# A fused AdaLN attention and FP4 feed-forward block: quantizer slots from a table, an identity product issued earlier, and steps in a new order

## The chip, the cores and the metric

The kernel runs on one core of one Trainium2 chip. The metric is the device time of one execution in microseconds (us), median of the runs shown. The core's engines are TensorE (PE in the rows; its weight loads PEld), VectorE (DVE), ScalarE (ACT), GpSimd (POOL) and SyncE (SP). Each engine works through its own instruction stream in order, and they meet through semaphores.

## The reference, cut to what matters

The input x is 4 batches of 1024 tokens of 128 features in float32. `c` gives six modulation vectors per batch.

```
h = layernorm(x) * (1 + ca) + sa
q, k = l2norm(heads(h Wq)), l2norm(heads(h Wk));  v = heads(h Wv)      # 16 heads of 8
beta, fast, slow = sigmoid(h Wb), sigmoid(h Wfd + bfd), sigmoid(h Wsd + bsd)
flux = clip(sigmoid(silu(k beta Wtf1 + btf1) Wtf2 + btf2), .01, .99)
M_fast, M_slow = sums over all tokens of (k beta weight)^T (v beta), weight = exp(suffix sum of log decay)
x = x + ga * ((alpha q M_fast + (1 - alpha) q M_slow) Wo),  alpha = 0.5 + 0.3 flux
h = layernorm(x) * (1 + cb) + sb
f = silu(q4(h) q4(w_gate)^T) * (q4(h) q4(w_up)^T)                      # 352 wide
x = x + gb * (q4(f) q4(w_down)^T)
```

`q4` quantizes to FP4 and back: in blocks of 16 values, scale = max|.|/6, the quotient rounded to the grid 0, .5, 1, 1.5, 2, 3, 4, 6, times the scale.

## The kernel before, in words

The 4096 tokens are worked on as 16 pairs (of 2 times 128 tokens), four pairs to a batch. A table, `ORDER`, gives for each of four engines a written list of steps such as `F1:12` (step F1, pair 12); the engine's program is that list and nothing reorders it. A step's name stands on each engine that takes part in it.

- First part, all pairs: `XN` normalizes, `PX` transposes, `PP` is the product with all attention weights (496 columns) and its copies out by ScalarE, and per batch the gates: `GA` (ScalarE, functions exp and ln), `GD`, `GS`, `GE` (silu and tanh), `V0` to `V3` (the state), `GG`. `MB` makes the modulation vectors, `W1`, `W2`, `W3` quantize and transpose the feed-forward weights.
- Second part, per pair i: `O1`, `O2`, `O3` (attention output, added to x), `L1` (second layer norm; its result goes to `q_x` columns 704 to 959), quantize, `N4` (transpose), `F1` (gate and up products, silu, the product of both into `q_x` columns 0 to 703), quantize, `F3` (transposes), `F4` (down product plus x, copy out, store).
- The quantizer works by slots. Slot s takes the columns that it has in one go: `Q` (VectorE: block maximum, scale, reciprocal), `QR` (GpSimd: times reciprocal), `QA` (ScalarE: absolute value into the one PSUM tile `q_A`), `QT` (VectorE: two instructions that round), `QO` (GpSimd: times scale). `q_x`, `q_r`, `q_o` have two buffers, taken by s mod 2. The norm of pair i is in slot i+4 and its feed-forward vector in slot i+6, so a slot has norm i with vector i-2. Of the 18 slots (4 to 21) the first two hold a norm alone (256 columns), the last two a vector alone (704 columns), 14 hold both (960 columns).

PSUM: three banks `pa` for results that ScalarE copies out, taken in turn in the order of TensorE's list, two banks `pv` for those that VectorE reads, one `pg` for the gates. A product waits until the bank three places earlier in that list is free. ScalarE's function tables hold either the exp/ln set or the silu/tanh set; where the list needs the other set, line 526 loads it.

Of the kernel before, what the change touches and what calls it, by code (L numbers as in the profile page):

```python
# [11 lines left out]
P = 128  # L12
# [66 lines left out]
        P0:0 XN:0 MV:0 XN:1 XN:2 XN:3 SB:0 P0:1 P0:2 PP:0 PP:1 PP:2 GA:0 P0:3 PP:3 W0:0 GB:0 PP:4 W1:0 PP:5 GK:0
        PP:6 W2:0 GE:0 PP:7 GF:0 PP:8 GA:1 GB:1 GY:0 PP:9 GG:0 GK:1 GA:2 PP:10 PP:11 O1:0 O1:1 GE:1 O1:2 GF:1  # L80
        O3:0 GB:2 O3:1 GY:1 L1:0 PP:12 O1:3 GK:2 GG:1 L1:1 Q:4 O3:2 QT:4 O3:3 Q:5 L1:2 GF:2 O1:4 PP:13 L1:3 GE:2
        PP:14 O1:5 PP:15 QT:5 F1:0 GA:3 Q:6 GB:3 O3:4 O1:6 GK:3 GG:2 QT:6 L1:4 O3:5 F1:1 GY:2 Q:7 L1:5 F1:2 Q:8
        QT:7 O1:7 O3:6 GE:3 QT:8 O1:8 L1:6 F1:3 GF:3 O1:9 Q:9 F1:4 Q:10 QT:9 O3:7 O3:8 L1:7 QT:10 F1:5 Q:11 GG:3
# [1140 lines left out]
```

## Time and profile before

| | us |
|---|---|
| median of 3 runs (lowest, highest) | 214.57 (213.33, 214.69) |
| the profiled execution's own time | 214.73 |
| its span in the trace | 213.0 |
| busy in the span: PE, DVE, ACT, POOL | 185.1, 174.6, 144.6, 152.9 |

The rows below are of that one execution. A row of a timeline gives start, duration, engine, line, operation, output and input, how many instructions it merges, and in brackets the idle time before it with the instruction that ended it. The steps of the list can be told by their lines: 952 to 960 are `Q`, 475 is `QR`, 691 `QA`, 968 and 971 `QT`, 487 `QO`, 982 the VectorE half of `F1`, 1177 and 714 are `F3`, 1187 and 1189 `F4`.

### The profile page before, as it was taken

What the parts mean: (1) busy time and instruction counts of PE and PEld (TensorE: products, weight loads), DVE (VectorE), ACT (ScalarE), POOL (GpSimd) and SP (SyncE); (2) the same over time, 40 slices, a digit from 0 to 9 for tenths busy, and PEclk for the clock granted to TensorE, in tenths of its full rate; (3) what the DMA queues carried; (4) which work ended last, traced back from release to release, by engine and by line L of the source; (5) the groups of instructions that cost most, each with busy time, mean ns of one, the idle gap of its engine ahead of it and who ended that gap; (6) DMA issues with size and microseconds to landing.
All of it is one profiled execution on the core that took longest, in us unless ns stands there. A gap on an engine that the chain in (4) does not pass through costs nothing.

```text
span 213.0 us, 3498 instructions
## 1 busy us (share of the span) xinstructions
PE 185.1 (87%) x948; PEld 134.6 (63%) x948; DVE 174.6 (82%) x436; ACT 144.6 (68%) x326; POOL 152.9 (72%) x187
## 2 busy tenths in 40 slices
PE   2699959699999999879669999989999996989973
PEld 1544426366787748539538777868786683875863
DVE  3795998956898999999999999899998896876730
ACT  2369898998998999969753637655726456653741
POOL 6367353797688878979997975977867967666530
PEclk9999987999999999999999999999999999999999
DMA  6980000000000000000000100010001000010011
GB/s 166 247 211 5 0 2 0 5 0 0 0 5 0 0 0 2 0 0 5 25 0 0 29 0 25 2 29 0 25 11 42 0 25 25 3 51 26 3 49 49
DMA packets 11499, 5.66 MB, mean 27 GB/s; under 512 B 1684, under 2 KB 11352, under 8 KB 11480
## 3 DMA queue, kind: packets, MB, share of 16 engines
q1 hardware_dynamic: 11168, 5.31, 9.1%
q8 instruction: 8, 0.13, 0.3%
q10 hardware_dynamic: 312, 0.13, 0.2%
q14 instruction: 11, 0.09, 0.1%
HBM read 3.34 MB, written 2.10 MB: 26 GB/s over the span
## 4 chain that ended last, share of the span: by engine, by line
PE 49%; ACT 18%; issue 13%; POOL 9%; DVE 6%; DMA 2%; SPq 0%; POOLq 0%; DVEq 0%; ACTq 0%
PE pa L1089 10%; PE pa L1166 6%; PE pv L1168 5%; PE pa L1189 4%; PE pv L1130 4%; POOL q_o L487 3%; PE pg L1113 3%; POOL q_r L475 3%; PE pa L1177 3%; PE pa L1139 3%; DMA wmod_sb<-in_L_wmod_dram 2%; ACT L526 2%; PE pv L1149 2%; ACT xn L680 2%; PE pa L1187 2%
## 5 line engine op out<-in xcount | busy, mean ns | idle before, releaser
L475 POOL TENSOR_TENSOR q_r<-q_x,q_rs 128x960 f32<-128x960 f32 (+2 forms) x18 | 29.6, 1644 | 14.4 <-DVE q_rs L960 14.3
L1089 PE MATMUL pa<-wcat,hT 128*128 128x496 f32 x64 | 32.2, 631 | 5.4 <-ACT sq L606 3.6
L487 POOL TENSOR_TENSOR q_o<-q_r,q_sp 128x960 f32<-128x960 f32 (+2 forms) x18 | 29.5, 1642 | 7.3 <-DVE q_r L971 6.4
L1166 PE MATMUL pa<-guT,hqT 128*128 128x352 f32 x64 | 25.3, 477 | 4.8 <-ACT hqT L697 4.7
L1189 PE MATMUL pa<-wdg,fqT 128*128 128x128 f32 x192 | 26.7, 275 | 0.0
L706 ACT ACTIVATE sgl<-pa 128x352 f32<-128x352 f32 x32 | 14.5, 461 | 15.1 <-PE pa L1166 12.9
L1168 PE MATMUL pv<-guT,hqT 128*128 128x352 f32 x64 | 24.3, 462 | 0.3 <-DVE oc L913 0.3
L438 POOL TENSOR_TENSOR vs<-kvg,cw 128x256 f32<-128x256 f32 x32 | 20.0, 651 | 5.8 <-DVE cw L864 5.8
L1189 PEld LDWEIGHTS pa<-wdg,fqT 128*128 128x128 f32 x192 | 24.0, 192 | 0.0
L1089 PEld LDWEIGHTS pa<-wcat,hT 128*128 128x128 f32 x64 | 12.0, 205 | 16.8 <-ACT sq L606 7.1
L691 ACT ACTIVATE q_A<-q_r 128x960 f32<-128x960 bf16 (+2 forms) x18 | 16.0, 888 | 8.3 <-POOL q_r L475 5.3
L982 DVE TENSOR_TENSOR q_x<-sgl,pv 128x352 f32<-128x352 f32 x32 | 15.7, 511 | 5.9 <-PE pv L1168 5.0
L968 DVE SCALAR_TENSOR_TENSOR q_x<-q_A,q_r 128x960 f32<-128x960 f32 (+2 forms) x18 | 18.5, 1026 | 2.5 <-ACT q_A L691 2.4
L952 DVE TENSOR_REDUCE q_am<-q_x 128x60 f32<-128x960 f32 (+2 forms) x18 | 18.7, 1039 | 1.0 <-POOL q_x L466 0.6
L971 DVE SCALAR_TENSOR_TENSOR q_r<-q_A,q_x 128x960 f32<-128x960 f32 (+2 forms) x18 | 18.8, 1046 | 0.6
L1166 PEld LDWEIGHTS pa<-guT,hqT 128*128 128x128 f32 x64 | 11.0, 189 | 11.3 <-ACT hqT L697 7.4
L1130 PE MATMUL pv<-wm,hT 128*128 128x256 f32 x64 | 16.5, 385 | 1.9 <-DVE q_x L982 1.7
L714 ACT ACTIVATE fqT<-pa 128x384 f32<-128x384 f32 x32 | 13.9, 486 | 6.1 <-PE pa L1177 6.1
L603 ACT ACTIVATE kvg<-pa 128x368 f32<-128x368 f32 x32 | 15.2, 475 | 3.8 <-PE pa L1089 3.1
L1168 PEld LDWEIGHTS pv<-guT,hqT 128*128 128x128 f32 x64 | 12.0, 190 | 7.6 <-DVE oc L913 1.2
L680 ACT ACTIVATE xn<-x_all,nmrb,rstdb 128x128 f32<-128x128 f32 x32 | 13.9, 485 | 3.2 <-DVE nmrb L941 3.0
L462 POOL TENSOR_TENSOR q_x<-xn,mb 128x256 f32<-128x256 f32 x16 | 11.8, 739 | 5.5 <-issue 5.1
(149 smaller groups left out, 447.5 us busy)
## 6 DMA issues: line engine op xcount, KB each, us to landing
out_dram<-x_all SPq DMA_DIRECT2D x16, 128.0 KB, 1.8
x_all<-in_L_attn_x_dram SPq DMA_DIRECT2D x3, 512.0 KB, 5.6
x_all<-in_L_attn_x_dram SPq DMA_DIRECT2D x2, 256.0 KB, 3.1
wmod_sb<-in_L_wmod_dram SPq DMA_DIRECT2D x1, 256.0 KB, 5.7
wraw<-in_L_ffn_w_down_dram SPq DMA_DIRECT2D x1, 176.0 KB, 4.5
wmod_sb<-in_L_wmod_dram SPq DMA_DIRECT2D x1, 128.0 KB, 5.2
wraw<-in_L_ffn_w_gate_dram SPq DMA_DIRECT2D x1, 128.0 KB, 3.2
wraw<-in_L_ffn_w_up_dram SPq DMA_DIRECT2D x1, 128.0 KB, 2.9
```

The source lines that it names most:

```text
L438: g.tensor_tensor(vs[:, t].rearrange("p a (h d) -> p a h d", d=DK), vt.unsqueeze(1).to_broadcast([P, 2, H, DK]), cw[:, t].unsqueeze(3).to_ ...
L475: g.tensor_tensor(blocks(q_r[:, s % 2, c]), blocks(q_x[:, s % 2, c]), spread(q_rs[:, s % 2, n]), ALU.mult)\
L487: g.tensor_tensor(blocks(q_o[:, s % 2, c]), blocks(q_r[:, s % 2, c]), spread(q_sp[:, s % 2, n]), ALU.mult)\
L680: a.activation(xn2[:, i % 2, k, :], x_all[:, b, 2 * j + k, :], ACT.Identity, scale=rstdb[:, i % 2, k:k + 1], bias=nmrb[:, i % 2, k:k + 1]) ...
L952: v.tensor_reduce(q_am[:, r, n], blocks(q_x[:, r, c]), axis=AX.X, op=ALU.max, apply_absolute_value=True)\
L968: v.scalar_tensor_tensor(q_x[:, r, c], q_A[:, c], MAGIC_FLOOR, q_r[:, r, c], ALU.max, ALU.add)\
L971: v.scalar_tensor_tensor(q_r[:, r, c], q_A[:, c], MAGIC_FLOOR, q_x[:, r, c], ALU.max, ALU.subtract, reverse1=True).then_inc(S["q_q"], 1)
L1089: te.matmul(bank_a(("PP%d" % k, i))[:, 0:NCAT], hT[:, b, 2 * j + k, :], wcat[:, :], start=True, stop=True).then_inc(S["a_full"], 1)
L1130: last = te.matmul(t[:, k * 2 * D:(k + 1) * 2 * D], hT[:, b, 2 * j + k, :], wm[:, b % 2, :], start=True, stop=True)
L1166: te.matmul(bank_a(("G%d" % k, i))[:, 0:I], lhs, guT[:, 0, :], start=True, stop=True)\
L1168: te.matmul(bank_v(("U%d" % k, i))[:, 0:I], lhs, guT[:, 1, :], start=True, stop=True)\
L1189: last = te.matmul(t[:, k * D:(k + 1) * D], fqT[:, (2 * i + k) % 4, ch * P:(ch + 1) * P], wdg[:, b % 2, ch, :], start=False, stop=(ch == 2))
```

## The change: what it does, and the diff

1. The slots come from a table, `SLOTS`. Norms 0 and 1 are alone in slots 0 and 1, slots 2 to 13 hold norm i with vector i-2 as before, norms 14 and 15 now stand alone in slots 14 and 15, and vectors 12 to 15 alone in slots 16 to 19. There are 20 slots: four of 256 columns, twelve of 960, four of 704. `before(s, part)` finds the slot that last used the same buffer for that part.
2. In `F4` TensorE's identity product of the first half (it adds x) no longer waits for ScalarE's copies of `F3`; the first half then waits for copy FT0 and the second for FT1. Before, all waited for FT1.
3. All four lists of `ORDER` are new. Of the table one line for one engine stands here.

```
-        P0:0 P0:1 KC:0 XN:4 XN:5 XN:6 P0:2 XN:7 P0:3 GO:0 XN:8 XN:9 GC:0 XN:10 GB:0 V0:0 GO:1 XN:11 V1:0 V2:0
+        KC:0 P0:0 P0:1 XN:4 XN:5 XN:6 P0:2 XN:7 GC:0 XN:8 XN:9 GO:0 GB:0 XN:10 XN:11 V0:0 V1:0 V2:0 V3:0 GF:0
...
-Q_NORM, Q_FFN = 4, 6
...
+        SLOTS = [(i, i - 2 if i >= 2 else None) for i in range(14)] + [(14, None), (15, None)] + [(None, i) for i in range(12, 16)]
+        norm_slot = {n: s for s, (n, _) in enumerate(SLOTS) if n is not None}
+        ffn_slot = {f: s for s, (_, f) in enumerate(SLOTS) if f is not None}
+
         def quant_span(s):
-            lo = 0 if s - Q_FFN >= 0 else QF0
-            return slice(lo, QCOLS if s - Q_NORM < PAIRS else QF0), slice(...)
+            n, f = SLOTS[s]
+            lo, hi = 0 if f is not None else QF0, QCOLS if n is not None else QF0
+            return slice(lo, hi), slice(lo // BLOCK, hi // BLOCK)
+
+        def before(s, part):
+            return max((p for p in range(s) if p % 2 == s % 2 and SLOTS[p][part] is not None), default=None)
...
             def QO(s):
-                if 0 <= s - 2 - Q_NORM < PAIRS:
-                    pool.wait_ge(S["a_full"], slot_a[("HQT", s - 2 - Q_NORM)] + 1)
-                if s - 2 - Q_FFN >= 0:
-                    pool.wait_ge(S["a_full"], slot_a[("FT1", s - 2 - Q_FFN)] + 1)
+                for part, bank in ((0, "HQT"), (1, "FT1")):
+                    p = before(s, part)
+                    if SLOTS[s][part] is not None and p is not None:
+                        pool.wait_ge(S["a_full"], slot_a[(bank, SLOTS[p][part])] + 1)
...
             def F4(i):
                 v_done(("Y", i))
-                a_done(("FT1", i))
-                pe.wait_ge(S["wdg"], b + 1)
                 for k in range(2):
                     te.matmul(t[:, k * D:(k + 1) * D], ident[:, :], x_all[:, b, 2 * j + k, :], start=True, stop=False)
+                    a_done(("FT%d" % k, i))
+                    if k == 0:
+                        pe.wait_ge(S["wdg"], b + 1)
                     for ch in range(3):
```

How the lists move the work is shown at three places. First, ScalarE at the first gate step of batch 0, between the copies of `PP:3` and of the pairs after it, before:

```order
L606 ACTIVATE sq<-pa 128x256
L590 ACTIVATE hT<-pa,colmod 128x256
L555 ACTIVATE mb<-pa 128x512 x4
L590 ACTIVATE hT<-pa,colmod 128x256
L603 ACTIVATE kvg<-pa 128x368
```

and with the change:

```order
L611 ACTIVATE sq<-pa 128x256
L531 ACT_TABLE_LOAD
L620 ACTIVATE eg<-zb 128x384
L623 ACTIVATE rn<-ss 128x256
L625 ACTIVATE rn<-rn,ln 128x256
L629 ACTIVATE lg<-eg 128x384
L631 ACTIVATE lg<-lg 128x384
L635 ACTIVATE lf<-lg,tiny 128x256
L560 ACTIVATE mb<-pa 128x512 x4
L595 ACTIVATE hT<-pa,colmod 128x256
```

The table load and the six activations of `GA:0` now stand ahead of the four copies of `MB:0`; before they came behind these, the `hT` copies of `PX:6` and `PX:7`, `PP:4` and `WQ:0`.

Second, VectorE's last steps, from the vector product of pair 12 on, before:

```order
L982 TENSOR_TENSOR q_x<-sgl,pv 128x352 x2
L952 TENSOR_REDUCE q_am<-q_x 128x60
L957 TENSOR_SCALAR q_sp<-q_am 128x60
L960 RECIPROCAL q_rs<-q_sp 128x60
L982 TENSOR_TENSOR q_x<-sgl,pv 128x352 x2
L952 TENSOR_REDUCE q_am<-q_x 128x60
```

and with the change:

```order
L961 RECIPROCAL q_rs<-q_sp 128x16
L981 TENSOR_TENSOR q_x<-sgl,pv 128x352 x2
L967 SCALAR_TENSOR_TENSOR q_x<-q_A,q_r 128x256
L970 SCALAR_TENSOR_TENSOR q_r<-q_A,q_x 128x256
L953 TENSOR_REDUCE q_am<-q_x 128x16
L958 TENSOR_SCALAR q_sp<-q_am 128x16
L961 RECIPROCAL q_rs<-q_sp 128x16
L953 TENSOR_REDUCE q_am<-q_x 128x44
L958 TENSOR_SCALAR q_sp<-q_am 128x44
L961 RECIPROCAL q_rs<-q_sp 128x44
L967 SCALAR_TENSOR_TENSOR q_x<-q_A,q_r 128x256
L970 SCALAR_TENSOR_TENSOR q_r<-q_A,q_x 128x256
```

The norms of pairs 14 and 15 are small slots of their own (16 blocks) beside vector 12's slot (44 blocks), where two slots of 60 blocks stood.

Third, TensorE's last step, `F4:15`, with the semaphores that its instructions wait for, before:

```order
L1187 MATMUL pa<-x_all,ident 128x128 [waits s_a_free,s_wdg,s_v_free]
L1189 MATMUL pa<-wdg,fqT 128x128 x3
L1187 MATMUL pa<-x_all,ident 128x128
L1189 MATMUL pa<-wdg,fqT 128x128 x3
L130 UNCONDITIONAL_BRANCH
```

and with the change:

```order
L1184 MATMUL pa<-x_all,ident 128x128 [waits s_v_free,s_a_free]
L1189 MATMUL pa<-wdg,fqT 128x128 [waits s_wdg,s_a_free]
L1189 MATMUL pa<-wdg,fqT 128x128 x2
L1184 MATMUL pa<-x_all,ident 128x128
L1189 MATMUL pa<-wdg,fqT 128x128 [waits s_a_free]
L1189 MATMUL pa<-wdg,fqT 128x128 x2
L130 UNCONDITIONAL_BRANCH
```

The wait for the copies (s_a_free of FT0 and FT1) has moved from the identity product to the three products behind it.

## Rows read from the trace of the kernel before

**Rows 1.** The page's first part: busy us of each engine, share, instructions.

```profile
PE 185.1 (87%) x948; PEld 134.6 (63%) x948; DVE 174.6 (82%) x436; ACT 144.6 (68%) x326; POOL 152.9 (72%) x187
```

**Rows 2.** Windows of 20 us: length, busy of each engine (instructions), granted clock, DMA.

```profile
20.00:40.00 20.00, 15.07 (x45) 7.89 (x45) 18.46 (x45) 18.15 (x40) 8.86 (x15) 0.91 0.00 0
40.00:60.00 20.00, 19.78 (x88) 13.50 (x87) 14.53 (x32) 18.71 (x47) 16.66 (x27) 1.00 0.01 1
60.00:80.00 20.00, 19.77 (x92) 14.27 (x91) 18.00 (x61) 18.46 (x49) 16.30 (x26) 1.00 0.00 1
80.00:100.00 20.00, 17.64 (x92) 13.40 (x91) 19.45 (x45) 16.87 (x34) 17.56 (x20) 1.00 0.00 1
...
180.00:200.00 20.00, 18.39 (x111) 13.96 (x110) 14.89 (x24) 11.50 (x26) 12.49 (x11) 1.00 0.08 21
```

**Rows 3.** Timeline of TensorE, 20 to 42 us: MB:0 and two waits.

```profile
19.32 3.67 PE L1061 MATMUL pa<-wmod_sb,scB 128*128 128x512 f32 x8
...
31.19 2.02 PE L1089 MATMUL pa<-wcat,hT 128*128 128x496 f32 x2 [2.65 <-ACT sq L606]
...
39.51 1.90 PE L1089 MATMUL pa<-wcat,hT 128*128 128x496 f32 x4 [1.74 <-ACT hT L590]
```

**Rows 4.** Windows of TensorE around the first of these waits: busy, granted clock, DMA.

```profile
29.00:31.00 2.00, 0.00 (x0) 0.94 0.00 0
31.00:32.00 1.00, 0.81 (x1) 0.50 0.00 0
...
34.00:35.00 1.00, 1.00 (x8) 0.91 0.00 0
```

**Rows 5.** Timeline of ScalarE: step GA:0 with its table load.

```profile
26.00 0.29 ACT L546 ACTIVATE wqT<-pa 128x128 f32<-128x128 f32 x1
26.30 1.28 ACT L526 ACT_TABLE_LOAD   x1
27.60 0.52 ACT L615 ACTIVATE eg<-zb 128x384 f32<-128x384 f32 x1
...
29.99 0.51 ACT L630 ACTIVATE lf<-lg,tiny 128x256 f32<-128x256 f32 x1
```

**Rows 6.** Timeline of VectorE in the tail: products of F1, slots 20 and 21.

```profile
179.34 0.52 DVE L982 TENSOR_TENSOR q_x<-sgl,pv 128x352 f32<-128x352 f32 x1 [1.22 <-PE pv L1168]
...
194.33 0.52 DVE L982 TENSOR_TENSOR q_x<-sgl,pv 128x352 f32<-128x352 f32 x1 [0.61 <-PE pv L1168]
194.88 0.89 DVE L952 TENSOR_REDUCE q_am<-q_x 128x44 f32<-128x704 f32 x1
...
196.02 0.43 DVE L960 RECIPROCAL q_rs<-q_sp 128x44 f32<-128x44 f32 x1
...
199.82 0.83 DVE L968 SCALAR_TENSOR_TENSOR q_x<-q_A,q_r 128x704 f32<-128x704 f32 x1
...
202.46 0.89 DVE L968 SCALAR_TENSOR_TENSOR q_x<-q_A,q_r 128x704 f32<-128x704 f32 x1 [0.89 <-ACT q_A L691]
...
203.39 0.89 DVE L971 SCALAR_TENSOR_TENSOR q_r<-q_A,q_x 128x704 f32<-128x704 f32 x1
```

**Rows 7.** Timeline of VectorE in slot 4, a norm alone.

```profile
67.30 0.42 DVE L952 TENSOR_REDUCE q_am<-q_x 128x16 f32<-128x256 f32 x1
...
67.97 0.25 DVE L960 RECIPROCAL q_rs<-q_sp 128x16 f32<-128x16 f32 x1
...
69.37 0.42 DVE L968 SCALAR_TENSOR_TENSOR q_x<-q_A,q_r 128x256 f32<-128x256 f32 x1
69.83 0.42 DVE L971 SCALAR_TENSOR_TENSOR q_r<-q_A,q_x 128x256 f32<-128x256 f32 x1
```

**Rows 8.** Timeline of the last steps: F4:14, F3:15, F4:15 and the copy out.

```profile
204.81 0.46 PE L1187 MATMUL pa<-x_all,ident 128*128 128x128 f32 x2 [0.84 <-ACT fqT L714]
...
206.67 0.82 PE L1177 MATMUL pa<-ident,q_o 128*128 128x128 f32 x6
...
207.20 0.87 ACT L714 ACTIVATE fqT<-pa 128x384 f32<-128x384 f32 x2
...
208.32 0.46 PE L1187 MATMUL pa<-x_all,ident 128*128 128x128 f32 x2 [0.84 <-ACT fqT L714]
...
210.38 0.38 ACT L720 ACTIVATE x_all<-pa 128x256 f32<-128x256 f32 x1 [2.31 <-PE pa L1189]
```

More of the change, by code:

```diff
@@ L77 @@
         F3:15 F4:15""",
     "vector": """
[L79 to L83, printed above, removed]
@@ L459, in L1 @@
                 pool.wait_ge(S["xn2"], 2 * i + 2)
-                if i >= 2:
-                    pool.wait_ge(S["q_q"], nth(i + Q_NORM - 2))
-                g.tensor_tensor(q_x[:, (i + Q_NORM) % 2, QF0:QCOLS].rearrange("p (t d) -> p t d", t=2), xn2[:, i % 2], mb[:, b, 2, :].unsqueeze(1).to_broadcast([P, 2, D]),
+                if before(norm_slot[i], 0) is not None:
+                    pool.wait_ge(S["q_q"], nth(before(norm_slot[i], 0)))
+                g.tensor_tensor(q_x[:, norm_slot[i] % 2, QF0:QCOLS].rearrange("p (t d) -> p t d", t=2), xn2[:, i % 2], mb[:, b, 2, :].unsqueeze(1).to_broadcast([P, 2, D]),
                                 ALU.mult).then_inc(S["u"], 1)
                 pool.wait_ge(S["u"], i + 1)
-                h2 = q_x[:, (i + Q_NORM) % 2, QF0:QCOLS].rearrange("p (t d) -> p t d", t=2)
+                h2 = q_x[:, norm_slot[i] % 2, QF0:QCOLS].rearrange("p (t d) -> p t d", t=2)
                 g.tensor_tensor(h2, h2, mb[:, b, 1, :].unsqueeze(1).to_broadcast([P, 2, D]), ALU.add).then_inc(S["h2"], 1)
             def QR(s):
-                if nth(s) < 1:
-                    return
                 c, n = quant_span(s)
@@ L944, in Q @@
             def Q(s):
-                if nth(s) < 1:
-                    return
                 r, (c, n) = s % 2, quant_span(s)
-                if s - Q_FFN >= 0:
-                    dve.wait_ge(S["v_free"], slot_v[("U1", s - Q_FFN)] + 1)
-                if s - Q_NORM < PAIRS:
-                    dve.wait_ge(S["h2"], s - Q_NORM + 1)
+                if SLOTS[s][1] is not None:
+                    dve.wait_ge(S["v_free"], slot_v[("U1", SLOTS[s][1])] + 1)
+                if SLOTS[s][0] is not None:
+                    dve.wait_ge(S["h2"], SLOTS[s][0] + 1)
                 v.tensor_reduce(q_am[:, r, n], blocks(q_x[:, r, c]), axis=AX.X, op=ALU.max, apply_absolute_value=True)\
@@ L974, in F1 @@
             def F1(i):
-                r = (i + Q_FFN) % 2
-                if i + Q_FFN - 2 >= Q_NORM:
-                    dve.wait_ge(S["q_q"], nth(i + Q_FFN - 2))
+                r = ffn_slot[i] % 2
+                if before(ffn_slot[i], 1) is not None:
+                    dve.wait_ge(S["q_q"], nth(before(ffn_slot[i], 1)))
                 for k in range(2):
@@ L1153, in N4 @@
             def N4(i):
-                pe.wait_ge(S["q_o"], nth(i + Q_NORM))
+                pe.wait_ge(S["q_o"], nth(norm_slot[i]))
                 t = bank_a(("HQT", i))
                 for k in range(2):
-                    last = te.transpose(t[:, k * D:(k + 1) * D], q_o[:, (i + Q_NORM) % 2, QF0 + k * D:QF0 + (k + 1) * D], ident[:, :])
+                    last = te.transpose(t[:, k * D:(k + 1) * D], q_o[:, norm_slot[i] % 2, QF0 + k * D:QF0 + (k + 1) * D], ident[:, :])
                 last.then_inc(S["a_full"], 1)
@@ L1171, in F3 @@
             def F3(i):
-                pe.wait_ge(S["q_o"], nth(i + Q_FFN))
+                pe.wait_ge(S["q_o"], nth(ffn_slot[i]))
                 for k in range(2):
@@ L1176, in F3 @@
                         o = k * I + CH[ch]
-                        last = te.transpose(t[:, ch * P:(ch + 1) * P], q_o[:, (i + Q_FFN) % 2, o:o + P], ident[:, :])
+                        last = te.transpose(t[:, ch * P:(ch + 1) * P], q_o[:, ffn_slot[i] % 2, o:o + P], ident[:, :])
                     last.then_inc(S["a_full"], 1)
```

69 lines of the change are left out of this document (34 added, 35 removed).

## The prediction, made before the changed kernel ran

> **What bounds the kernel now.** I read the page's busy totals first, then windows of 20 us, then each engine's timeline where the windows show a gap. By the totals [rows 1] TensorE has the most work, 185.1 of 213.0 us, and VectorE 174.6, too close to name one bound for all. The windows [rows 2] tell the stages apart. From 40 to 80 us TensorE is busy 39.55 of 40 us and ScalarE 37.17: nothing that isn't taken off TensorE helps there, and ScalarE has 2.83 us to spare. From 80 us on VectorE is nearest to full (19.45 of 20), TensorE waits 2.36 us in 20. From 180 us on neither is full (VectorE 14.89 of 20): what limits there is the way round, from one quantizer slot through `N4`, `F1` and the next-but-one slot. The page's chain of waits hops between all four engines there, which says the same.
>
> In the start stretch, 20 to 40 us, TensorE is idle 4.93 us [rows 2], most of it in two waits: 2.65 us while ScalarE runs the gate step `GA:0`, and 1.74 us behind `GS:0` [rows 3]. After the first the granted clock is 0.50 until about 34 us [rows 4]: the 1.2 GHz level instead of 2.4, after two microseconds with no product at all. Some 3 us of products at half speed lost about 1.5 us.
>
> **The change, term by term.** All sums start from the profiled execution: span 213.0, own time 214.73, which is 0.16 above the median of 214.57.
>
> *The slots of the tail.* Before, norms 14 and 15 wait to be quantized with vectors 12 and 13, so `F1:14` can't begin before vector 12 exists, though it doesn't need it. With the change they go alone. I count VectorE's new list from its first product of `F1:12`, which starts at 179.34 [rows 6], since all ahead of it is the same in kind. Prices: `F1`, two products paced by TensorE 0.52 + 0.61 + 0.52 = 1.65, or 1.09 where TensorE is ahead (both 0.52 and a start gap, an estimate from the same row); `Q` of a vector alone 194.88 to 196.45, 1.57; its `QT` 0.83 and 0.89 back to back, 199.82 to 201.57, 1.75 [rows 6]; `Q` of a norm alone 67.30 to 68.22, 0.92, and its `QT`, 69.37 to 70.25, 0.88 [rows 7]. The list reads F1:12, QT:14, Q:15, Q:16, QT:15, which is 1.65 + 0.88 + 0.92 + 1.57 + 0.88 = 5.90; then three times F1, Q, QT, which is 3 x (1.09 + 1.57 + 1.75) = 13.23; then the wait for `QA` (there is one `q_A`) 0.89 and the last `QT` 1.82 (202.46 to 204.28) [rows 6]. Together 21.84: the last `QT` ends at 201.18 instead of 204.28, **3.1 us earlier**. `Q:14` adds 0.92 ahead of `F1:12`, in the 1.22 us that VectorE idles there; if that cover is gone (GpSimd late with norm 14's `L1`), it costs up to 0.92. This sum has VectorE never waiting otherwise. TensorE is not full there either, beside VectorE's 4.41 us per vector (`F1`, `F3`, `F4` and `N4`, of which `F4` takes 1.78 by the next term), and GpSimd's `QR` and `QO` of a vector are about as long as `Q` and `QT` together less the reduction; each hop between them can still show. Bounds: 0 (all of it returned as waits, since VectorE gets more slots to do, each with its own fixed part: 0.92 + 0.88 for 256 columns against 1.57 + 1.75 for 704) and 4.0. I take 3.1 here and keep 1.0 off as a margin below.
>
> *The identity product.* In `F4:15` the first product starts at 208.32, 0.25 us after the second copy ended at 207.20 + 0.87 = 208.07; the eight products issue in 1.78 us (F4:14 starts at 204.78 by its weight load, F3:15 follows at 206.56 in the same way; the rows of the products are 204.81 and 206.67) [rows 8], 0.22 each. The first copy ends about 0.43 before the second. Now the first half goes at 207.64 + 0.25 = 207.89 without its identity product, ends at 208.56, the second identity product at 208.78, the last three at 209.45 instead of 210.07: **0.6 us** for `F4:15`, and **0.6** more for `F4:14`, because `F3:15` stood behind it on TensorE: its input came from the `QT` that ended at 204.28 plus `QO` and was there by 205.8, yet it began at 206.67 [rows 6, 8]. For the 14 pairs before, the product is work that fills an idle moment where there is one and costs nothing where there isn't. Bounds 0.6 and 1.3; I take 1.2.
>
> *The order at the start.* `WK:0` moves behind `CM:0`: one small copy and transpose in front of the first `PX`, at most 0.3 us. `GA:0` moves in front of the copies of `MB:0`. By its rows it holds ScalarE from 26.30 to 30.50, 4.2 us [rows 5]. `MB:0` has four products in 3.67 us [rows 3], and three banks: TensorE can run three, some 2.7 us, and then waits for a copy that stands behind `GA:0`. The wait is then some 3 us in place of 2.65. At the old place of `GA:0` no wait remains, so the net is 0 to +0.6, and I take +0.3. At `GS:0`, `WQ:0` and the copies of `PP:7` now stand ahead of it, so TensorE has `GE:0` and `PP:8` to do while ScalarE is away: of the 1.74 us wait [rows 3] about half should go, -0.9 (bounds 0 and -1.7).
>
> *Two more table loads.* The new ScalarE list changes the function set 12 times, the old one 10. A load is 1.28 us [rows 5]: 2.57 us more on ScalarE before 80 us, where it has 2.83 us to spare and TensorE none [rows 2]. `W3:0` (nine copies) leaves that stretch for the one behind `N4:0`, which makes room. Hidden fully 0, not at all +2.6; I take half, +1.3. The rows show the load beginning as the copy before it ends (26.29) and the exp 0.02 us behind it [rows 5].
> The Trainium skill, "ScalarE: Activation LUTs", section "What ACT_TABLE_LOAD costs", gives a switch as a load of 1283 ns plus a drain of about 1380 ns, 2.66 us in all. By it the two loads would be 5.3 us and this term up to 2.7 us larger; the trace agrees on the load and shows no drain here.
>
> *The rest of the order.* The middle, 80 to 180 us, is rearranged by a few places everywhere. VectorE is nearly full there and its work is unchanged, so I give it 0, with bounds of -2 and +2 (half of what TensorE idles in the window from 80, on either side, twice over).
>
> Sum: -3.1 + 1.0 (hops) - 1.2 + 0.3 + 0.3 - 0.9 + 1.3 = -2.3. The terms that I halved (table loads, `GS:0`) lean to the good side, since ScalarE also gives up `W3:0` in that stretch, worth nine copies; I take another 0.8 for it. **-3.1 us**: 214.57 - 3.1 = 211.5.
>
> **The rivals.**
>
> *A: ScalarE binds from 40 to 80 us (0.25).* For it: 37.17 busy us of 40, plus 2.57. Against: `W3:0` moves out. The start then costs +0.6 + 2.6, the tail gives 2.1 + 1.2: -0.1, time 214.5.
>
> *B: slower, the clock falls more often (0.13).* Place: TensorE's wait behind `GA:0`, now in front of `MB:0`'s copies, and those behind `GS:0` and `GA:1`, which follow it sooner. Before, a wait of 2.65 us was followed by 0.50 of the clock for some 3 us, the 1.74 us wait by none [rows 3, 4]. From the point where one or both of the later waits are as long as the first, each costs about 1.5 us more beside its own added 0.9. Two of them +4.8, the tables +2.6, start +0.6, tail -3.3: +4.7 at worst, and with one of them +2.3: time 216.9, up to 219. TensorE is full until 80 us, so none of it is won back there.
>
> *C: the waits in the middle go as well (0.15).* The first long wait is broken up by `MB:0`'s products, so the clock keeps 2.4 GHz (-1.5), and earlier `O1` and `O3` steps feed VectorE sooner (-1.5 of the 2.36 us of TensorE's waits per 20 us from 80 us on [rows 2]): time 208.5.
>
> *D, inside my forecast's range:* the identity product does its part and the slots don't, because GpSimd, with two more slots, takes the place of the way round: 214.57 - 1.2 and the start terms (+0.3 + 0.3 - 0.9 + 1.3 - 0.8 = +0.2), 213.6.
>
> **How the numbers follow.** The forecast, 211.5, has 0.47; A 0.25, B 0.13, C 0.15. The range takes the forecast with its bounds and most of A and C: 208.9 to 215.0. About 1% (2.1 us) is what a measurement of this kernel can tell from no change. Faster than 212.4: three quarters and more of the forecast's 0.47, C's 0.15, a little of A, together 0.58. Within 1%: the rest of the forecast and of A and a bit of B, 0.30. Slower: 0.12.
>
> **What would show it.** In the profile of the changed kernel: VectorE's last `QT` some 3 us earlier counted from `F1:12`, with idle moments between 180 and 200 us down from 5.1 us to about 2; TensorE's identity products at 1184 starting without an idle bracket from `fqT`, and the last one ahead of the copy's end; 12 table loads; ScalarE near 19.5 of 20 us from 40 to 80 if A holds; the granted clock at 0.50 in more than one stretch if B does, in none if C does. What would make me wrong most easily is the start: every microsecond lost before 80 us is carried to the end.

## The result

The changed kernel takes 218.0 us (median of 4 executions, 215.81 to 218.26) against 214.3 for the kernel before on the same chip: ratio 1.016, 95% interval 1.009 to 1.023. Forecast were 211.5 us and a range up to 215.0, so it is slower where the prediction had it faster. The profiled execution took 218.26 us, its span is 216.5, 3.5 more than before.

### The profile page after: what moved, and what is told of

It reads as the page before. It is cut to its first block, busy times and chain, and to the rows that moved or that the text cites. A ratio compares the mean times of both kernels' runs of the same rounds, so it can differ in the third digit from the quotient of the medians.

```text
span 216.5 us, 3524 instructions
## 1 busy us (share of the span) xinstructions
PE 187.3 (86%) x948; PEld 136.3 (63%) x948; DVE 182.7 (84%) x446; ACT 146.2 (68%) x330; POOL 154.5 (71%) x191
## 4 chain that ended last, share of the span: by engine, by line
PE 35%; ACT 17%; DVE 16%; POOL 16%; issue 12%; DMA 2%; SPq 0%; POOLq 0%; DVEq 0%; ACTq 0%
PE pa L1088 7%; PE pa L1165 6%; POOL q_r L482 5%; PE pv L1167 4%; POOL q_o L492 4%; ACT L531 3%; PE pv L1129 3%; PE pa L1189 3%; DVE q_r L970 2%; DVE q_am L953 2%; DVE q_x L967 2%; DMA wmod_sb<-in_L_wmod_dram 2%; ACT kvg L608 2%; DVE hz L874 2%; POOL q_x L471 2%
## 5 line engine op out<-in xcount | busy, mean ns | idle before, releaser
L1088 PE MATMUL pa<-wcat,hT 128*128 128x496 f32 x64 | 30.5, 605 | 1.0 <-ACT sq L611 1.0
L1165 PE MATMUL pa<-guT,hqT 128*128 128x352 f32 x64 | 26.3, 494 | 5.0 <-ACT hqT L700 4.9
L1167 PE MATMUL pv<-guT,hqT 128*128 128x352 f32 x64 | 25.7, 485 | 1.1 <-DVE x_all L926 0.7
L411 POOL TENSOR_SCALAR xn<-x_all,nmean,rstd 128x128 f32<-128x128 f32 x24 | 13.5, 573 | 10.8 <-PE pa L1078 10.5
L447 POOL TENSOR_TENSOR vs<-kvg,cw 128x256 f32<-128x256 f32 x32 | 19.5, 636 | 1.5 <-DVE cw L867 1.5
L1167 PEld LDWEIGHTS pv<-guT,hqT 128*128 128x128 f32 x64 | 12.5, 199 | 9.4 <-DVE oc L916 1.4
L1165 PEld LDWEIGHTS pa<-guT,hqT 128*128 128x128 f32 x64 | 11.5, 198 | 10.3 <-ACT hqT L700 6.1
L1112 PE MATMUL pg<-vs,kvg 128*128 128x256 f32 x64 | 16.9, 399 | 0.0
```

The lines of the kernel that those rows point to most:

```text
L1088: te.matmul(bank_a(("PP%d" % k, i))[:, 0:NCAT], hT[:, b, 2 * j + k, :], wcat[:, :], start=True, stop=True).then_inc(S["a_full"], 1)
L1165: te.matmul(bank_a(("G%d" % k, i))[:, 0:I], lhs, guT[:, 0, :], start=True, stop=True)\
L1167: te.matmul(bank_v(("U%d" % k, i))[:, 0:I], lhs, guT[:, 1, :], start=True, stop=True)\
```

## The profile after

First the page's busy totals, in the form of [rows 1], and its line of the granted clock in 40 slices:

```profile
PE 187.3 (86%) x948; PEld 136.3 (63%) x948; DVE 182.7 (84%) x446; ACT 146.2 (68%) x330; POOL 154.5 (71%) x191
...
PEclk9999999699999999759999999999999999999999
```

VectorE is busy 8.1 us longer, though the two added slots are worth some 2 us (176.5 in the version with the old lists up to `F1:10`, below, which has them too). The clock falls at two places. The windows that answer to [rows 2]:

```profile
20.00:40.00 20.00, 15.09 (x54) 8.28 (x53) 16.88 (x43) 19.38 (x46) 10.65 (x18) 0.97 0.01 2
40.00:60.00 20.00, 18.23 (x77) 12.77 (x77) 16.61 (x34) 16.36 (x37) 11.04 (x16) 0.95 0.00 0
60.00:80.00 20.00, 19.05 (x87) 12.76 (x85) 17.92 (x54) 19.66 (x50) 17.26 (x25) 1.00 0.01 1
80.00:100.00 20.00, 15.74 (x61) 10.96 (x61) 16.73 (x38) 11.96 (x25) 14.80 (x20) 0.83 0.00 0
...
180.00:200.00 20.00, 19.69 (x126) 15.78 (x125) 17.45 (x33) 13.27 (x32) 15.81 (x15) 1.00 0.10 28
```

TensorE was full from 40 to 80 us before (39.55 us); now it has 37.28 there, and 15.74 instead of 17.64 in the window from 80. The last window is better: 19.69 for 18.39, and VectorE 17.45 for 14.89.

To say where time goes, both kernels are cut at the same two points of work: VectorE's first product of `F1:0` and that of `F1:10`. The vector steps ahead of each are the same in both lists. Windows of the kernel before, from 20 us:

```profile
20.00:80.80 60.80, 55.43 (x226) 36.20 (x226) 51.75 (x138) 56.11 (x135) 42.56 (x66) 0.97 0.00 1
80.80:165.80 85.00, 76.86 (x436) 59.66 (x435) 79.93 (x178) 54.41 (x115) 70.48 (x71) 1.00 0.04 12
165.80:213.00 47.20, 38.66 (x251) 30.82 (x249) 30.65 (x50) 23.49 (x52) 28.03 (x23) 1.00 0.09 26
```

and after:

```profile
20.00:83.30 63.30, 55.63 (x228) 36.01 (x227) 54.60 (x135) 57.48 (x138) 42.17 (x63) 0.97 0.00 1
83.30:172.90 89.60, 79.26 (x431) 60.81 (x431) 82.52 (x177) 52.47 (x111) 71.93 (x75) 0.96 0.03 10
172.90:216.50 43.60, 38.44 (x254) 31.48 (x253) 32.10 (x62) 24.35 (x56) 28.44 (x25) 1.00 0.11 31
```

The start is 2.5 us longer (TensorE idle 7.67 us for 5.37), the middle 4.6 longer, the tail 3.6 shorter: +3.5, the whole difference. I call these three start, middle and tail.

TensorE's longest waits in the new start and middle, from its timeline:

```profile
23.45 1.12 PE L1060 MATMUL pa<-wmod_sb,scB 128*128 128x512 f32 x2 [2.54 <-ACT mb L560]
...
38.86 0.45 PE L1077 MATMUL pa<-ident,xn 128*128 128x128 f32 x1 [2.37 <-ACT sq L611]
...
48.20 1.90 PE L1088 MATMUL pa<-wcat,hT 128*128 128x496 f32 x4 [1.01 <-ACT sq L611]
...
91.15 1.54 PE L1165 MATMUL pa<-guT,hqT 128*128 128x352 f32 x2 [4.18 <-ACT hqT L700]
```

and short windows of TensorE behind the second and the last of them (busy, granted clock, DMA):

```profile
39.00:40.00 1.00, 1.00 (x4) 0.50 0.00 0
...
90.00:91.00 1.00, 0.00 (x0) 0.50 0.00 0
...
95.00:96.00 1.00, 1.00 (x3) 0.50 0.00 0
```

After the wait of 2.54 us the clock stayed up; after 2.37 and after 4.18 us it went to 0.50, the 1.2 GHz level. The products of `F1:1` take 1.54 and 1.38 us at that level; those of `F1:0`, at 2.4 GHz, took 0.76. The second of these falls lasts 6.8 us, twice as long as the first.

The tail on VectorE, which answers to [rows 6]:

```profile
187.76 0.47 DVE L981 TENSOR_TENSOR q_x<-sgl,pv 128x352 f32<-128x352 f32 x1
...
193.85 1.00 DVE L981 TENSOR_TENSOR q_x<-sgl,pv 128x352 f32<-128x352 f32 x2
...
207.54 0.89 DVE L967 SCALAR_TENSOR_TENSOR q_x<-q_A,q_r 128x704 f32<-128x704 f32 x1 [0.89 <-ACT q_A L694]
208.46 0.89 DVE L970 SCALAR_TENSOR_TENSOR q_r<-q_A,q_x 128x704 f32<-128x704 f32 x1
```

From the first product of `F1:12` to the end of the last `QT` are 21.59 us, before 24.94. And the last steps, which answer to [rows 8]:

```profile
211.49 0.87 ACT L717 ACTIVATE fqT<-pa 128x384 f32<-128x384 f32 x2
211.62 0.47 PE L1184 MATMUL pa<-x_all,ident 128*128 128x128 f32 x2
212.03 0.94 PE L1189 MATMUL pa<-wdg,fqT 128*128 128x128 f32 x6
...
213.90 0.38 ACT L723 ACTIVATE x_all<-pa 128x256 f32<-128x256 f32 x1 [1.54 <-PE pa L1189]
```

The identity product begins 0.13 us after the copies begin, without an idle bracket; the last copy out waits 1.54 us for its product, not 2.31.

## Single executions come in steps

One fact is needed to read the runs. Every kernel here is measured in executions with different mean granted clocks, and its time goes by them. The kernel before took 212.0 to 213.1 us in the executions with a clock of 1.000 and 213.2 to 215.3, mostly 213.8 to 214.9, in those with 0.992; both kinds occur side by side on one chip. An execution with one fall is thus some 2.0 us longer. The changed kernel had no execution above 0.984: its four were 218.26 (0.975), 218.04 (0.976), 217.96 and 215.81 (0.984). Medians stand below, and the clock where it decides.

The fall itself is only half of the 2.0 us. Nine profiles (that of b4_both, below, left out) show the start of the kernel before, with its wait of 2.65 us for `GA:0`. In four of these profiles the clock fell behind that wait, in five it did not. A row of such an execution without a fall (c4_before_stt), which answers to the second row of [rows 3]:

```profile
29.68 1.10 PE L1098 MATMUL pa<-wcat,hT 128*128 128x496 f32 x2 [2.65 <-ACT sq L611]
```

From the end of the wait to VectorE's first product of `F1:0` the five take 48.7 us and the four 49.7 to 49.9: the fall costs 1.0 us there. The rest lies ahead of it: the wait ends at 29.6 to 30.2 us in the five and at 30.4 to 31.2 in the four. A fall at another place also makes a mean of 0.992 (86 us in b2_oldstart, 176 us in a1_ident).

## Experiments: the parts of the change by themselves

**The identity product alone**, in the kernel before:

```
-                a_done(("FT1", i))
-                pe.wait_ge(S["wdg"], b + 1)
                 for k in range(2):
                     te.matmul(... ident[:, :], x_all[:, b, 2 * j + k, :] ...)
+                    a_done(("FT%d" % k, i))
+                    if k == 0:
+                        pe.wait_ge(S["wdg"], b + 1)
```

> The kernel before with one edit, the identity product of F4 ahead of the copies' wait. Theory (the tail is bound by the way round, the last two F4 lie in it): 0.6 us for F4:15 and up to 0.6 for F4:14, so 1.2 us faster than before, about 213.1. Rival (the product only moves an idle moment, and the last copy is late for another reason): no change, within 0.3 us.

Measured 211.56 us, ratio 0.990 (0.984 to 0.995). At equal clock: 210.6 to 210.7 against some 212.35 at 1.000, and 212.5 against 214.4 at 0.992, so 1.7 to 1.9 us.

**The new slots with the new lists of the tail only.** The new lists begin at `N4:11` (TensorE, ScalarE), `F1:10` (VectorE) and `QR:12` (GpSimd), with the old order ahead; with and without the identity product:

```
-    new lists throughout
+    old lists up to F1:10, then the new ones; SLOTS as in the change
```

> The changed kernel's slots, identity product and the last part of its lists (from N4:11 on TensorE, F1:10 on VectorE), behind the lists of before for all that comes ahead. Theory (the change gains in the tail what was forecast and loses it in the part ahead of it): 4 to 5 us faster than before, 209.3 to 210.3. Rival (the tail only looks shorter in the changed kernel because its pairs arrived late and waiting work had piled up): 213 or more.

> As the run with slots and tail, but F4 waits for both copies before its identity product, as before. Theory: 1.2 us behind that run, about 211, so slots and tail order alone give 3.1 to 3.7 us. Rival (the two parts overlap, each alone gives most of it): within 0.4 us of that run.

209.69 us, ratio 0.980 (0.974 to 0.986), and without the identity product 211.34, 0.990 (0.986 to 0.994). In both profiles the last `QT` ends 21.59 us behind the first product of `F1:12`, and from there to the end it is 7.16 us with the identity product issued earlier and 9.05 without. So what it gives lies wholly behind the last `QT`. Both parts of the change do what they were to do, and their gains add up: at a clock of 1.000 the kernel with both takes 208.7 to 209.0, 3.4 us less than the kernel before. All that is lost lies in the order ahead of pair 10.

**The reverse**: the new lists up to `F1:9`, the old slots and the old tail.

> The slots of before, the changed kernel's lists up to F1:9, the lists of before behind that, identity product in its new place. Theory (the new order ahead of the tail costs some 7 us, by the vector product of pair 10 that starts at 172.9 instead of 165.8): 219 to 222. Rival (the new order of the head costs nothing by itself, the loss comes from the slots): within 2 us of before.

Median of four 221.58 us, ratio 1.026 (1.017 to 1.035). This kernel has the identity product too, so the kernel to set it against is the one before with that product alone, 211.56: even its two fastest executions, 218.82 and 220.03, lie 7.3 and 8.5 us above it. That agrees with the 8.3 us between the changed kernel and the one with the old order ahead (218.0 and 209.69).

## Experiments: where in the order

**The old lists up to `F1:0`**, the new ones behind:

> The changed kernel with the lists of before up to F1:0 (GA:0 behind MB:0, GS:0 ahead of PX:9, the two table loads gone), its own lists behind. Theory (the new start brings F1:0 2.5 us later): 2 to 3 us faster than the changed kernel, 215 to 216, the 4.2 us wait ahead of F1:1 still there. Rival (TensorE and VectorE catch up behind the start, nothing of it reaches the end): within 1 us of the changed kernel.

211.86 us, ratio 0.994 (0.990 to 0.998), 6.1 below the changed kernel, more than both theories had. The windows of its start and middle:

```profile
20.00:78.30 58.30, 52.45 (x224) 34.68 (x223) 50.05 (x131) 54.69 (x133) 39.29 (x60) 1.00 0.00 1
78.30:166.40 88.10, 78.60 (x433) 60.28 (x432) 81.75 (x177) 52.82 (x112) 72.93 (x76) 0.98 0.04 10
```

The start is 5.0 us shorter than in the changed kernel and 2.5 shorter than before; the latter is no gain of the lists, which are the same, but an execution without a fall there. The middle takes 88.1, still 3.1 above before, with a fall behind a wait of 2.52 us for `hqT`.

**The old lists up to `F1:5`:**

> The lists of before up to F1:5, the changed kernel's behind that, new slots and identity product. It cuts the middle in two: with the changed lists from F1:0 on the time was 211.9, with them from N4:11 on 209.7. Theory (the loss sits at F1:1, where VectorE and TensorE wait behind GA:3): 209.4 to 210.2. Rival (it sits between F1:6 and F1:10): 211.3 to 212.3.

212.5 us, ratio 0.993 (0.990 to 0.996); the version with the cut at `F1:10` has 209.69. The theory that the middle's loss sits at `F1:1` falls: some 2.8 us are lost between `F1:6` and `F1:10`. The middle of the version with the cut at `F1:10`, and that of this one:

```profile
80.20:164.70 84.50, 76.73 (x435) 59.61 (x434) 79.29 (x177) 54.10 (x115) 70.45 (x71) 1.00 0.04 12
```

```profile
80.70:168.10 87.40, 77.25 (x433) 59.46 (x432) 81.30 (x177) 53.38 (x112) 70.66 (x72) 1.00 0.04 10
```

Both are at full clock, and VectorE has 177 instructions in both, yet it is busy 2.0 us longer in the second: of the 2.9 us that the middle grows by, 2.0 are instructions of VectorE that last longer (more on these below), 0.9 its idle time. The next run's middle takes 87.1 us at full clock with the new lists from the start on. So at full clock `F1:0` to `F1:5` lose nothing more; what they add in the changed kernel is the fall of the clock.

**Dummy products in TensorE's wait for `F1:1`**, 16 identity products into the bank that comes next (their results are overwritten):

```
+                if i == 1:
+                    t = bank_a(("G0", i))
+                    for _ in range(16):
+                        te.matmul(t[:, 0:P], ident[:, :], ident[:, :], start=True, stop=True)
```

> The changed kernel with 16 products of the identity matrix with itself (128x128, result not used, into the bank that F1:1 fills next) ahead of F1:1's wait on TensorE. It leaves the wait for the copy in place and gives TensorE some 3.5 us of work in it. Theory (half of the loss there is the clock at 0.50 behind the wait): no fall of the clock between 88 and 97 us, F1:1 as late as in the changed kernel but at full speed, 2 to 3 us faster, 215 to 216. Rival (the clock falls alone cost nothing since VectorE sets the pace): same time as the changed kernel, or slower by what the products cost.

216.52 us, ratio 1.014 (1.009 to 1.020), 1.5 below the changed kernel. TensorE's timeline and the window of the middle:

```profile
87.48 3.73 PE L1163 MATMUL pa<-ident 128*128 128x128 f32 x32
91.83 0.86 PE L1169 MATMUL pa<-guT,hqT 128*128 128x352 f32 x2 [0.61 <-ACT hqT L700]
```

```profile
84.00:171.10 87.10, 80.37 (x463) 62.94 (x462) 82.36 (x177) 52.41 (x111) 71.81 (x75) 1.00 0.04 10
```

VectorE's and ScalarE's part of it is as late as ever, but the clock holds at 1.00 and the middle is 2.5 us shorter than the 89.60 of the changed kernel. That part of the 4.6 us is the clock; 2.1 are left that aren't. Against before (85.00 us, 79.93 busy) VectorE is busy 2.4 us longer here and idle no longer. The whole kernel gains less than 2.5 us, since this execution has a fall more at the start.

**`N4:1`'s copy ahead of `GA:3` on ScalarE**, alone and with the old start:

```
-  PP:15 N4:0 W3:0 GE:2 F1:0 L1:3 O2:4 GA:3 QA:2 N4:1 F1:1
+  PP:15 N4:0 W3:0 GE:2 F1:0 L1:3 O2:4 N4:1 GA:3 QA:2 F1:1
```

> The changed kernel with one step moved: on ScalarE the copy N4:1 stands ahead of the gate step GA:3 instead of behind it and QA:2. Theory (F1:1 on TensorE now stands ahead of V2:2, O2:5 and the rest, and waits 4.2 us for that copy; the clock falls behind the wait): wait and fall go, 3 to 6 us faster than the changed kernel, 212 to 215. Rival (VectorE, full there, sets the pace, the wait only stores what comes later): under 1.5 us faster.

> Both moves: the lists of before up to F1:0, and the copy N4:1 ahead of GA:3, the rest as in the changed kernel. Theory: the two causes add up, 7 to 8 us faster than the changed kernel, 209.5 to 211, level with before's lists and the new tail (209.7). Rival (a third cause sits between 100 and 170 us): 212 or more.

218.07 us (1.022, 1.016 to 1.027): no gain. The wait of 4.18 us is gone, but 2.82 us stand in its place one step on, for VectorE's `O3`, and the clock fell there as well. With the old start 215.7 (1.005, 1.000 to 1.009), worse than the old start alone; its only profile is of an execution of 467.93 us and says nothing on why.

## Experiments: VectorE's held instructions

The new profile shows VectorE instructions that last many times their usual length. The timeline of all engines, at `GE:0` and `V0` to `V3` of batch 0:

```profile
37.10 4.74 POOL L447 TENSOR_TENSOR vs<-kvg,cw 128x256 f32<-128x256 f32 x8
...
38.12 4.44 DVE L874 TENSOR_SCALAR hz<-hmid,wtf_b 128x128 f32<-128x128 f32 x1 [1.73 <-ACT hmid L654]
...
42.59 1.40 DVE L877 SCALAR_TENSOR_TENSOR hz<-hmid,wtf_b,hz 128x128 f32<-128x128 f32 x3
...
44.95 0.42 ACT L623 ACTIVATE rn<-ss 128x256 f32<-128x256 f32 x1 [2.85 <-DVE ss L835]
```

The first `hz` takes 0.33 us in eight other profiles. Here GpSimd has eight instructions back to back, and `hz` ends behind them and the `mrt` that follows. ScalarE's `GA:1`, which needs the sums behind `hz`, waits 2.85 us. Another case, in the middle:

```profile
162.64 1.82 POOL L492 TENSOR_TENSOR q_o<-q_r,q_sp 128x960 f32<-128x960 f32 x1
162.74 1.74 DVE L944 SCALAR_TENSOR_TENSOR nmrb<-mvb,rstdb 128x2 f32<-128x2 f32 x1
```

Four values per partition, 0.15 us elsewhere, end with GpSimd's instruction. By each kind's usual duration (an estimate from the rows) VectorE is held some 14 us in the changed kernel and some 6 before; of the added 8, 4.1 are the `hz` above. Between `F1:6` and `F1:10` two `nmrb` and a `q_sp` (1.74, 0.89 and 0.73 us for 0.15, 0.15 and 0.19) are held 2.9 us in all, and the same three in the run with the old lists up to `F1:5`; before, all that is held there is 0.5 us. So one more theory: the new order is slow because it puts GpSimd's long instructions beside VectorE's short ones.

**Another form of the instruction** for the first `hz`, then for all single-source steps on the way (`hz`, `rt`, `yt`, `q_sp`), in the changed kernel, the fastest one and the one before:

```
-  v.tensor_scalar(hz[:, :, :], hmid[:, :, :, 0], wtf2_b[:, 0:1], None, ALU.mult)
+  v.scalar_tensor_tensor(hz[:, :, :], hmid[:, :, :, 0], wtf2_b[:, 0:1], zt[:, :, :], ALU.mult, ALU.add)
```

> The changed kernel with one VectorE instruction written otherwise: the first one on hz (TENSOR_SCALAR, 128x128) becomes SCALAR_TENSOR_TENSOR with a tile of zeros as third operand, the form that the next three on hz have. In the changed kernel its first instance took 4.44 us (the others 0.33) while GpSimd ran nine instructions back to back, in three profiles alike. Theory (VectorE is held off from SBUF by GpSimd in that form, PP:7's sums and with them GA:1 on ScalarE come late, and the start loses by it): the instance takes 0.4 to 0.7 us, ScalarE's 2.85 us wait in GA:1 goes, 2.5 to 4 us faster than the changed kernel, 214 to 215.5. Rival (the start loses through its table loads and GA:0 ahead of MB:0, VectorE has slack there): within 1 us of the changed kernel.

> The changed kernel with all four such VectorE instructions written so (first of hz, the sum's reciprocal input rt, the clip of yt, and q_sp of each quantizer slot). In the changed kernel two of rt took 1.6 instead of 0.18 us and three of q_sp 0.5 to 0.73 instead of 0.19. Theory: another 0.5 to 1.5 us faster than with hz alone, 213 to 214.5. Rival (only the first hz lay on the path): equal to the run with hz alone.

> The kernel with the lists of before, the new slots and tail and the identity product (209.7), with the four instructions written so. Theory (VectorE is nearly full from 80 us on, and six q_sp there took 0.48 to 0.87 instead of 0.19): 0.5 to 1.5 us faster, 208.2 to 209.2. Rival (the waits lie where VectorE would wait anyway): no change, 209.7.

> The kernel before with the four instructions written so. No hz instance takes over 0.75 us there. Theory: little to take away, 0.3 to 1.2 us faster, 213.1 to 214. Rival (the form itself is faster or slower by its reads and not by what GpSimd holds): as large a change as in the changed kernel.

218.36 (1.026), 219.36 (1.025), 211.29 (0.989) and 213.12 (0.998, 0.994 to 1.002): none is faster than its kernel without the edit (the last was mostly at a clock of 1.000, where it takes 212.6 to 213.4 us and the kernel before 212.0 to 213.1), and the first `hz` takes 4.47 us in the new form too. The form isn't it.

**GpSimd made to leave a gap**: `V1:0` waits for the first `hz`.

```
+                if b == 0 and n == 1:
+                    pool.wait_ge(S["hz"], 1)
```

> The changed kernel with one wait added: GpSimd holds its second pair of state products of batch 0 (V1:0) until VectorE's first instruction on hz is done, so the nine GpSimd instructions that held that instruction off for 4.4 us no longer run in one row. Theory (VectorE is held off while GpSimd's instructions follow each other without a gap, whatever the form of its own): the instruction takes under 0.8 us, ScalarE's 2.85 us wait in GA:1 goes, 2 to 3.5 us faster than the changed kernel (218), 214.5 to 216. Rival (the hold-off is real but the start is bound elsewhere, by table loads and ScalarE): hz is short and the time is within 1 us of the changed kernel.

```profile
24.31 2.08 PE L1062 MATMUL pa<-wmod_sb,scB 128*128 128x512 f32 x2 [2.78 <-ACT mb L562]
...
40.42 0.33 DVE L876 TENSOR_SCALAR hz<-hmid,wtf_b 128x128 f32<-128x128 f32 x1 [1.71 <-ACT hmid L656]
...
41.15 0.45 PE L1079 MATMUL pa<-ident,xn 128*128 128x128 f32 x1 [2.37 <-ACT sq L613]
```

The hold is gone (0.33 us), and so is the wait of 1.01 us at 48 us. `MB:0`'s wait was 2.78 us instead of 2.54, and this time the clock fell there too: its two products took 2.08 us, not 1.12. Three falls, 218.3 us (1.018, 1.013 to 1.023). From the wait for `sq` to the first product of `O2:0` 1.3 us were won, and by then 2.3 had been lost. So the hold costs 1.3 us there; in the total another fall hides it.

**Five held steps moved by a place or two** on VectorE (`GF:2`, `GA:3`, `GF:3`, `L1:10`, `L1:12`), in the changed kernel:

```
-  ... O1:13 F1:7 L1:10 Q:9 ... QT:10 O1:14 L1:12 F1:9 Q:11
+  ... O1:13 F1:7 Q:9 L1:10 ... QT:10 O1:14 F1:9 L1:12 Q:11
```

> The changed kernel with five steps of VectorE's list moved by one or two places, so that five short instructions which its profile shows held behind a long GpSimd instruction (1.57 to 1.85 us in place of 0.18 to 0.56) start elsewhere: GF:2 behind QT:1, GA:3 behind Q:2, GF:3 behind Q:6, L1:10 behind Q:9, L1:12 behind F1:9. Held time in all: 1.43 + 1.29 + 1.39 + 0.74 + 1.59 = 6.4 us of VectorE, 3.7 of it between F1:3 and F1:10. Theory 1 (the middle of the new order costs what VectorE is held there): the stretch from F1:3 to F1:10 falls from 60.8 to about 57.5 us, the held rows are 0.2 to 0.6, and the kernel gains 2 to 4 us, 214 to 216 us. Theory 2 (the middle is slow by the way round through TensorE and ScalarE, and the held time lies in what would be idle): the rows get short, VectorE idles instead, and the time is 217 to 219 us. Theory 3 (other short instructions are held in their place): VectorE's busy sum stays at 182 to 183 us, and so does the time.

219.4 us (216.60 to 222.91), ratio 1.021 (1.015 to 1.026). Its middle:

```profile
82.30:172.60 90.30, 78.36 (x437) 61.36 (x436) 80.65 (x178) 52.15 (x111) 72.11 (x75) 0.96 0.03 10
```

VectorE is busy 177.2 us in all, not 182.7, and nothing is won in total. Nearest is Theory 2, though the median lies above its range. But most of these 5.5 us are not the moved steps. 4.1 are the first `hz`, which none of the moves touches; its rows:

```profile
37.70 5.04 POOL L447 TENSOR_TENSOR vs<-kvg,cw 128x256 f32<-128x256 f32 x8
...
38.77 0.33 DVE L874 TENSOR_SCALAR hz<-hmid,wtf_b 128x128 f32<-128x128 f32 x1 [1.70 <-ACT hmid L654]
```

Here `hz` got in at once, beside the same chain of GpSimd without a gap. It began 0.14 us before the end of the GpSimd instruction that ran, in the held cases 0.17 to 0.20 before; that this decides is not shown. From the wait for `sq` to the first product of `O2:0` this execution takes 9.95 us, the run with the dummy products 11.05: again 1.1 us for the hold.

In the middle, which is busy 1.9 us less and takes 0.7 longer, the stretch from `F1:6` to `F1:10`, where `L1:10` and `L1:12` moved, takes 34.9 us for 35.6; from `F1:0` to `F1:6`, where `GA:3` and `GF:3` moved, it takes 55.4 for 54.0. From `F1:3` to `F1:10` it is 61.3 us, not the 57.5 of Theory 1. So taking the hold away gave 0.7 us at one place, and the moves, or what followed from them, cost more than that at another. That the held time makes the new order slow is neither shown by this run nor excluded.

**In the fastest version** the same move for two steps, `L1:6` behind `F1:3` and `L1:14` behind `F1:11`:

> The fastest version so far (old order ahead of the last pairs, new slots and new order behind, 209.7 us), with L1:6 moved behind F1:3 and L1:14 behind F1:11 on VectorE. Its profile shows L1:6's instruction held from 106.8 for 1.58 us instead of 0.15, right ahead of F1:3, and L1:14's for 0.72. Theory 1: VectorE's busy sum falls by 2.0 to some 174.5 us and the time by 0.5 to 2.0, to 207.7 to 209.2. Theory 2: L1 comes later by what F1 takes, GpSimd's L1 and the next Q with it, and nothing is won: 209.2 to 210.5.

208.73 us, ratio 0.976 (0.972 to 0.981), 1.0 less than without. Before the move and after it:

```profile
106.82 1.58 DVE L944 SCALAR_TENSOR_TENSOR nmrb<-mvb,rstdb 128x2 f32<-128x2 f32 x1
108.32 0.94 DVE L981 TENSOR_TENSOR q_x<-sgl,pv 128x352 f32<-128x352 f32 x2
```

```profile
105.57 0.52 DVE L981 TENSOR_TENSOR q_x<-sgl,pv 128x352 f32<-128x352 f32 x1
...
106.92 0.15 DVE L944 SCALAR_TENSOR_TENSOR nmrb<-mvb,rstdb 128x2 f32<-128x2 f32 x1
```

At a clock of 0.999 and 1.000 it takes 207.42 and 207.70, the other 208.66 to 208.97, so some 1.3 us at equal clock. Before the move the hold stood right in front of `F1:3`, on a VectorE with 79.32 busy of 84.60 us in the middle. This is the fastest kernel of the study.

## Experiments: single moves at the start

Both stand on the kernel with the gap in GpSimd. **Fewer table loads**: `GE:0` ahead of `GA:1`, `GS:1` behind `GD:1`, `GE:1` ahead of `GA:2`, 10 loads instead of 12. **`GA:0` behind `MB:0`** on ScalarE, as before:

```
-  GA:1 PP:9 GG:0 GE:0 PP:10 GS:1 PP:11 GD:1
+  GE:0 GA:1 PP:9 GG:0 PP:10 PP:11 GD:1 GS:1
```

```
-  PX:4 PP:3 GA:0 MB:0 PX:5
+  PX:4 PP:3 MB:0 GA:0 PX:5
```

> The run with the added wait, and on ScalarE GE:0 ahead of GA:1, GS:1 behind GD:1, GE:1 ahead of GA:2 (on VectorE GE:1 ahead of GA:2 too): 10 table loads instead of 12. Theory (ScalarE is nearly full to 80 us, two loads are 2.57 us of it): 1.5 to 2.6 us faster than the run with the wait alone. Rival (the loads are hidden): within 0.7 us of it.

> The run with the added wait, and on ScalarE the copies of MB:0 ahead of GA:0. Theory (GA:0 ahead of the copies stops TensorE for 2.5 us with its three banks full): 1 to 2.5 us faster than the run with the wait alone. Rival (GA:0 costs TensorE the same wait wherever it stands): within 0.7 us of it.

222.23 us (1.042, 1.037 to 1.048) and 220.78 (1.031, 1.026 to 1.036), at clocks of 0.954 to 0.961 and 0.961 to 0.977. Both are slower, and both have more of the clock at 0.50: 20 and 17 us in the profiles, where the kernel that they stand on has 10. With `GA:0` behind `MB:0` the wait there is 3.54 us, not 2.78. So putting back either step alone gains nothing; what the loads or the place of `GA:0` cost at an equal clock these two runs don't say.

## Why the prediction was wrong

**The step that failed** is "The middle, 80 to 180 us, is rearranged by a few places everywhere. VectorE is nearly full there and its work is unchanged, so I give it 0, with bounds of -2 and +2". The middle measured +4.6 us: 2.1 by the order and 2.5 by a fall of the clock behind TensorE's wait of 4.18 us for `hqT`. Two things were wrong in it. Unchanged work says nothing on when an input is there: in the new lists TensorE has 61 products between 80 and 100 us where it had 92, and stands before `F1:1` with nothing left to do. And the same instructions don't take the same time: VectorE has 177 in the middle for 178 before and is busy 82.52 us for 79.93, held beside GpSimd; the prediction has no term for that.

**The start**, forecast between +0.3 + 0.3 - 0.9 + 1.3 - 0.8 = +0.2 and A's +3.2, measured +2.5, with a fall in both kernels.
- `GA:0` ahead of `MB:0`: "some 3 us in place of 2.65"; it is 2.54. Right.
- `GS:0`: "of the 1.74 us wait [rows 3] about half should go". It grew to 2.37 us. (The 1.74 were short because TensorE came late out of the fall; in the five profiles of the old start without one this wait is 2.20 to 2.21.) `GE:0`, `WQ:0` and `PP:8` were done on TensorE at 36.5 us, when ScalarE was in `GS:0`, and the clock fell behind this wait, where before it had not. This term is 0.6 + 0.9 = 1.5 us off, and more by the clock.
- The held `hz`, with ScalarE's wait of 2.85 us behind it, has no term in the prediction; where it wasn't held, 1.1 and 1.3 us of the start were won.
- Two more table loads: ScalarE is busy 19.38 + 16.36 + 19.66 = 55.40 us from 20 to 80 us, before 55.32. `W3:0` paid for the loads, as the 0.8 had it. The load at 35.04 us takes 1.28 us and the next function begins 0.01 us behind it. The Trainium skill's "ScalarE: Activation LUTs", section "What ACT_TABLE_LOAD costs", adds a drain of about 1380 ns to a switch; no profile of this study shows one.
- A fall was priced at about 1.5 us; on the old start it costs 1.0 by itself.

**What was right.** The tail: forecast 21.84 us from `F1:12` to the last `QT`, measured 21.59, and the slots gave 1.7 to 2.0 us at equal clock, where 3.1 less the margin of 1.0 was entered. The margin was needed: from `F1:10` to `F1:12`, which the sum left out but for `Q:14`, it is 15.15 us with the new slots behind the old lists and was 13.57 before. The identity product gave 1.7 to 1.9 where 1.2 stood, above its bound of 1.3: the mechanism and the place, behind the last `QT`, were right, the size too small. Together 3.4 us against 3.3, so the sum fits better than its two terms.

**The rivals.** A doesn't hold: ScalarE has 36.02 of 40 us from 40 to 80, less than before. C is wrong, and D too, since the slots did their part. B comes nearest: its 216.9 up to 219 hold the 218.0, and the clock falls in more than one stretch, once behind `GS:0` as it said. But it charged all of this to the start; the other fall came at 90 us, and the order of the middle was no part of it. Its 0.13 was too small: [rows 3, 4] already showed one such wait with a fall behind it, and the change moved three of them.

**What stays open.** That the new order costs 2.1 us in the middle at full clock, all of it between `F1:6` and `F1:10`, and 2.3 us of TensorE's idle time at the start, is shown by cutting the lists and by the windows. That VectorE's held instructions are what makes those 2.1 us fits the busy time in three profiles (2.0 to 2.6 us longer with the same instructions), but the one run that took holds away there got 0.7 back. Whether a given wait brings the clock down also stays open: behind the wait at `MB:0` of 2.54 to 2.61 us it fell in two profiles (b3_filler, e1_unheld) and not in four, behind 2.78 it fell, and behind the same 2.65 us of the old start it fell in four profiles of nine.

## What to carry to other kernels

Test the parts of a change apart: here two good parts, 3.4 us, were buried under a new order that lost twice as much. Cut two orders at points of equal work and compare the stretches; it names the place in one run each. A wait of TensorE like the ones here (2.4 to 4.2 us) is to be priced twice, as time and as a possible fall of the clock (1.0 us at the start, 2.5 for the long one in the middle), and where medians differ by less than 2 us, executions should be compared at equal clock. Equal instructions in a new order need not take equal time: look at the busy sum of each stretch, not only at its idle time.
